# One graph layer on one core: the last bias of the message network moves from a TensorE product into the node part, by GpSimd, from the fifth group of nodes on

## The reference

```
h   = relu([x[src], x[dst]] @ Wm1 + bm1)      # 256 wide
h   = relu(h @ Wm2 + bm2)
agg = segment_mean(h @ Wm3 + bm3, dst)        # mean over the edges of a node, 0 where it has none
upd = relu([x, agg] @ Wn1 + bn1) @ Wn2 + bn2
out = layernorm(x + (x + upd))
```

## Time and profile before

| what | value |
|---|---|
| median of three runs | 1202.36 us (1200.36 to 1205.51) |
| the profiled execution: its own time | 1202.66 us |
| the profiled execution: span | 1200.9 us |
| busy share of the span: PE, PEld, DVE, ACT, POOL | 97%, 96%, 80%, 62%, 64% |
| last layer, from the first group's counts (1106.9) to the end | 94 us |

### The profile page before, as it was taken

One profiled execution on the slowest core, in us unless ns is written; L12 is line 12 of the kernel. 1 busy time (PEld: TensorE's weight loads), 2 busy tenths in 40 slices (PEclk: granted clock), 3 DMA queues, 4 the chain that ended last, 5 costly groups with the idle time before them and its releaser, 6 DMA issues.

```text
span 1200.9 us, 33955 instructions
## 1 busy us (share of the span) xinstructions
PE 1170.1 (97%) x9614; PEld 1149.9 (96%) x9615; DVE 961.7 (80%) x2072; ACT 747.9 (62%) x1392; POOL 770.2 (64%) x814
## 2 busy tenths in 40 slices
PE   6889999999999999999999999999999999999996
PEld 6778999999999999999999999999999999999886
DVE  6775877788788878888888888888888888888676
ACT  3555666666666666666666666666666666664684
POOL 2067777777777777777777777777777777771000
PEclk9998999999999999999999999999999999999999
DMA  9776666666665666666666666566666666662022
GB/s 327 274 289 176 181 179 175 179 181 177 180 178 178 178 180 177 179 177 179 178 179 179 180 178 179 176 180 177 180 179 176 179 180 178 179 177 75 27 71 92
DMA packets 135605, 211.42 MB, mean 176 GB/s; under 512 B 24247, under 2 KB 102669, under 8 KB 134030
## 3 DMA queue, kind: packets, MB, share of 16 engines
q0 software_dynamic: 37536, 102.55, 29.9%
q1 hardware_dynamic: 98030, 108.43, 29.4%
HBM read 188.09 MB, written 22.80 MB: 176 GB/s over the span
## 4 chain that ended last, share of the span: by engine, by line
PE 94%; DVE 1%; SPq 1%; DMA 1%; issue 1%; POOL 0%; ACT 0%; DVEq 0%
PE bank L1442 46%; PE bank L1418 14%; PE bank L1329 8%; PE sums L1352 4%; PE sums L1346 4%; PE sums L1350 4%; PE sums L1354 4%; PE bank L1483 3%; PE sums L1496 2%; PE bank L1239 1%; DMA a_table<-work 1%; PE bank L1466 1%; PE bank L1224 1%; PE sums L1224 1%; PE bank L1479 0%
## 5 line engine op out<-in xcount | busy, mean ns | idle before, releaser
L635 POOL DMA_INDIRECT a_edge<-a_table,src_idx x782 | 750.8, 960 | 258.9 <-issue 155.3
L1442 PE MATMUL bank<-w,h 128*128 128x256 f32 x4692 | 620.8, 282 | 0.0
L1442 PEld LDWEIGHTS bank<-w,h 128*128 128x128 f32 x4692 | 584.5, 189 | 0.0
L737 ACT ACTIVATE h<-bank 128x512 fp32r<-128x512 f32 x391 | 233.9, 598 | 324.7 <-PE bank L1329 321.8
L1111 DVE SCALAR_TENSOR_TENSOR h<-bank,h 128x512 fp32r<-128x512 f32 x391 | 269.4, 689 | 121.7 <-ACT h L737 85.7
L1123 DVE SCALAR_TENSOR_TENSOR h_lo<-bank,h_hi 128x512 fp32r<-128x512 f32 x391 | 266.7, 682 | 0.0
L726 ACT COPY bank<-b_bc 128x512 f32<-128x512 f32 x391 | 231.6, 592 | 42.9 <-DVE h_lo L1123 38.2
L1418 PE MATMUL bank<-ident,a_edge 128*128 128x128 f32 x1564 | 235.4, 273 | 5.7 <-DVE onehot_t L1028 3.9
L745 ACT ACTIVATE h_hi<-bank 128x512 fp32r<-128x512 f32 x391 | 232.9, 596 | 2.9 <-PE bank L1442 2.9
L1028 DVE TENSOR_SCALAR onehot_t<-rel,node_half 128x256 fp32r<-128x256 int16 x391 | 143.8, 368 | 57.8 <-DMA rel<-rel_dram 40.6
L1329 PE MATMUL bank<-onehot_t,b_win 128*128 128x256 f32 x782 | 189.9, 324 | 0.0
(11 more groups left out here) (190 smaller groups left out, 681.9 us busy)
## 6 DMA issues: line engine op xcount, KB each, us to landing
b_win<-b_table SPq DMA_DIRECT2D x391, 128.0 KB
rel<-rel_dram SPq DMA_DIRECT2D x196, 128.0 KB
a_edge<-a_table,src_idx POOLq DMA_INDIRECT x782
a_table<-work SPq DMA_DIRECT2D x12, 512.0 KB, 4.6
b_table<-work SPq DMA_DIRECT2D x5, 1024.0 KB, 6.0
b_table<-h SPq DMA_DIRECT2D x4, 1024.0 KB, 5.1
f_x<-in_x SPq DMA_DIRECT2D x12, 256.0 KB, 4.7
b_table<-a_edge SPq DMA_DIRECT2D x3, 1024.0 KB, 5.9
```

What stands on the lines that cost most here:

```text
L635: pool.indirect_dma_start(a_edge[:, b % R * TB + t, :], None, a_table, bass.IndirectOffsetOnAxis(ap=src_idx[:, b * TB + t:b * TB + t + 1], ...
L737: act.activation(h1[:, k % U, 0, :], bank[k % 2][:, :], ACT.Relu).then_inc(s_h1h, 1)
L1442: ins = pe.matmul(to, h1[:, j, a, h * EB + t * P:h * EB + (t + 1) * P], w2[:, b, h, :], start=False, stop=(a == 1 and h == KH - 1), skip_g ...
```

## The change

For groups 0 to 3 nothing changes in the arithmetic. From group 4 on (BY_ROW = 4) the mask row's transposes (L1467), its copy (L771) and its products with `b3_rows` (L1479) are left out. In their place `hx` itself gets mask times bm3 @ Wn1[128:256] added, by GpSimd, before ACT puts it into the banks. For that the mask of all nodes is made once (DVE), transposed (PE), copied (ACT), stored to DRAM by five transfers and loaded back spread over 128 partitions, 512 nodes at a time. The first three loads are issued by SP, the others by ACT. The diff, cut to its core:

```
+        b3_cols = sb("b3_cols", [P, KH * 2], F32)
+        f_mask, f_rows_by_4, f_rows = carve(P), carve(P), carve(P)
+        f_mask_bc = a_edge[:, 0:6, :].rearrange("p (k q) h -> p k (q h)", k=3)
+        BY_ROW = 4
+        def load_mask(e, g):
+            n = size(g) * P
+            e.dma_start(f_mask_bc[:, g % 3, 0:n], mask_dram[g * GW * P:g * GW * P + n].partition_broadcast(P)
+                        ).then_inc(s_mb[g % 3], 16)
 sync, behind the first three load_x_again:
+            whole = mask_dram[0:(NW - 1) * P].rearrange("(g n w a) -> w g n a", n=GW, w=GW, a=QUARTER)
+            sp.wait_ge(s_mc, 2)
+            for w in range(GW):
+                sp.dma_start(whole[w], f_rows_by_4[w:NW - 1:GW, :].rearrange("g (n a) -> g n a", n=GW)
+                             ).then_inc(s_ms, 16)
+            sp.dma_start(mask_dram[(NW - 1) * P:NW * P].rearrange("(o p) -> o p", o=1), f_rows[NW - 1:NW, :]
+                         ).then_inc(s_ms, 16)
+            sp.wait_ge(s_ms, 16 * (GW + 1))
+            for g in range(BY_ROW, BY_ROW + 3):
+                load_mask(sp, g)
 gpsimd, behind the gathers and the memsets of f_row (with f_mask cleared before them):
+            pool.wait_ge(s_hxa, 2 * NG)
+            pool.wait_ge(s_b3c, 1)
+            for g in range(BY_ROW, NG):
+                pool.wait_ge(s_mb[g % 3], 16 * mask_loads(g))
+                if g > BY_ROW:
+                    pool.wait_ge(s_hm, KH * (g - BY_ROW))
+                for h in range(KH):
+                    pool.tensor_scalar(f_part[h][:, 0:size(g) * P], f_mask_bc[:, g % 3, 0:size(g) * P],
+                                       b3_cols[:, 2 * h:2 * h + 1], None, ALU.mult).then_inc(s_hp, 1)
+                for h in range(KH):
+                    pool.wait_ge(s_hp, KH * (g - BY_ROW) + h + 1)
+                    at = hx[h][:, g * GW * P:(g * GW + size(g)) * P]
+                    pool.tensor_tensor(at, at, f_part[h][:, 0:size(g) * P], ALU.add).then_inc(s_hm, 1)
 scalar:
             def put_hx(g):
+                if g >= BY_ROW:
+                    act.wait_ge(s_hm, KH * (g - BY_ROW + 1))
+                    if size(g + 3):
+                        load_mask(act, g + 3)
...
-                    act.copy(f_row[g % 2][0:2, 0:n * P], bank[F_ROW][0:2, 0:n * P]).then_inc(s_fr, 1)
+                    if g < BY_ROW:
+                        act.copy(f_row[g % 2][0:2, 0:n * P], bank[F_ROW][0:2, 0:n * P]).then_inc(s_fr, 1)
+                    if g == 0:
+                        act.wait_ge(s_mt, 1)
+                        act.copy(f_rows_by_4[:, :]..., bank[F_UPD][:, 0:P]...).then_inc(s_mc, 1)
+                        act.copy(f_rows[:, :], bank[F_UPD][:, 0:P]).then_inc(s_mc, 1)
 vector, in copy_wc and behind means(0):
+                dve.tensor_copy(b3_cols[:, :], bank[0][:, 0:KH * 2]).then_inc(s_b3c, 1)
+            dve.tensor_scalar(f_mask[:, 0:NW], agg3[:, 0:NW, H:H + 1]..., 1.0, None, ALU.min).then_inc(s_mk, 1)
 tensor, beside the product of bm3 (L1297):
+                    for h in range(KH):
+                        pe.matmul(bank[0][:, 2 * h:2 * h + 2], wn1[:, 1, h * P:(h + 1) * P], b3_col[:, :],
+                                  start=True, stop=True)
 tensor, in the last layer:
-                        pe.wait_ge(s_fr, g)
+                        pe.wait_ge(s_fr, min(g, BY_ROW))
...
-                        ins = pe.transpose(by_nodes(bank[F_ROW][0:2, :], g, w), f_mean[:, k, w, H:HC], ident[:, :])
+                        if g < BY_ROW:
+                            ins = pe.transpose(by_nodes(bank[F_ROW][0:2, :], g, w), f_mean[:, k, w, H:HC],
+                                               ident[:, :])
...
                         keep_busy(bank[F_UPD][:, :], 9)
+                        pe.wait_ge(s_mk, 1)
+                        pe.transpose(bank[F_UPD][:, 0:P], f_mask[:, :], ident[:, :]).then_inc(s_mt, 1)
...
-                        pe.matmul(to, b3_rows[:, h * P:(h + 1) * P], f_row[j][:, 0:n], start=False, stop=False,
-                                  skip_group_check=True)
+                        if g - 1 < BY_ROW:
+                            pe.matmul(to, b3_rows[:, h * P:(h + 1) * P], f_row[j][:, 0:n], start=False, stop=False,
+                                      skip_group_check=True)
...
                     if g >= 3:
                         pe.wait_ge(s_fy, g - 2)
+                    else:
+                        pe.wait_ge(s_mc, 2)
```

More of the change, by code:

```diff
@@ L58, in gnn_layer @@
     rel_dram = nc.dram_tensor("rel_dram", [NB, EB], I16, kind="Internal").ap()
+    mask_dram = nc.dram_tensor("mask_dram", [NW * P], F32, kind="Internal").ap()
     mm_dram = nc.dram_tensor("mm_dram", [NB, 2], I32, kind="Internal").ap()
@@ L203, in gnn_layer @@
         f_row = [h1[:, k, 0, :] for k in range(2)]
+        f_mask, f_rows_by_4, f_rows = carve(P), carve(P), carve(P)
+        f_mask_bc = a_edge[:, 0:6, :].rearrange("p (k q) h -> p k (q h)", k=3)
+        f_part = (a_edge[:, 6:8, :].rearrange("p q h -> p (q h)"),
+                  rel[:, :, :].rearrange("p c e -> p (c e)").bitcast(F32))
+        BY_ROW = 4
         F_ROW, F_UPD = 5, 4
@@ L219, in gnn_layer @@
         s_b3 = sem("s_b3_parts")
+        s_b3c = sem("s_b3_columns")
         s_w2s = sem("s_w2_split")
@@ L293, in gnn_layer @@
         s_fr = sem("s_mask_row")
+        s_mz = sem("s_mask_zeroed")
+        s_mk = sem("s_mask_made")
+        s_mt = sem("s_mask_transposed")
+        s_mc = sem("s_mask_rows_copied")
+        s_ms = sem("s_mask_stored")
+        s_mb = [sem(f"s_mask_spread{k}") for k in range(3)]
+        s_hp = sem("s_masked_b3")
+        s_hm = sem("s_hx_with_masked_b3")
         s_fh = sem("s_hidden_product")
@@ L379, in f_hid, with mask_loads @@
             return agg[:, at:at + size(g) * P]
+        def mask_loads(g):
+            return sum(j % 3 == g % 3 for j in range(BY_ROW, g + 1))
+        def load_mask(e, g):
+            n = size(g) * P
+            e.dma_start(f_mask_bc[:, g % 3, 0:n], mask_dram[g * GW * P:g * GW * P + n].partition_broadcast(P)
+                        ).then_inc(s_mb[g % 3], 16)
         def by_dve(g):
@@ L638, in _ @@
                                             ).then_inc(s_g[b % R], 16)
+            pool.memset(f_mask[:, :], 0.0).then_inc(s_mz, 1)
             pool.wait_ge(s_w2, LAG)
@@ L770, in _ @@
                         act.wait_ge(s_frz, 2)
-                    act.copy(f_row[g % 2][0:2, 0:n * P], bank[F_ROW][0:2, 0:n * P]).then_inc(s_fr, 1)
+                    if g < BY_ROW:
+                        act.copy(f_row[g % 2][0:2, 0:n * P], bank[F_ROW][0:2, 0:n * P]).then_inc(s_fr, 1)
+                    if g == 0:
+                        act.wait_ge(s_mt, 1)
+                        act.copy(f_rows_by_4[:, :].rearrange("p (n a) -> p n a", n=GW),
+                                 bank[F_UPD][:, 0:P].rearrange("p (a n) -> p n a", n=GW)).then_inc(s_mc, 1)
+                        act.copy(f_rows[:, :], bank[F_UPD][:, 0:P]).then_inc(s_mc, 1)
                 n = size(g - 1)
@@ L1157, in _ @@
             means(0)
+            dve.wait_ge(s_mz, 1)
+            dve.tensor_scalar(f_mask[:, 0:NW], agg3[:, 0:NW, H:H + 1].rearrange("p w o -> p (w o)"), 1.0, None, ALU.min
+                              ).then_inc(s_mk, 1)
             for g in range(NG + 4):
@@ L1465, in _ @@
                         for h in range(KH):
-                            pe.transpose(by_nodes(bank[h], g, w), f_mean[:, k, w, h * P:(h + 1) * P], ident[:, :])
-                        ins = pe.transpose(by_nodes(bank[F_ROW][0:2, :], g, w), f_mean[:, k, w, H:HC], ident[:, :])
+                            ins = pe.transpose(by_nodes(bank[h], g, w), f_mean[:, k, w, h * P:(h + 1) * P],
+                                               ident[:, :])
+                        if g < BY_ROW:
+                            ins = pe.transpose(by_nodes(bank[F_ROW][0:2, :], g, w), f_mean[:, k, w, H:HC],
+                                               ident[:, :])
                     ins.then_inc(s_fmt, 1)
@@ L1474, in _ @@
                     pe.wait_ge(s_flo, 2 * g)
-                    pe.wait_ge(s_fr, g)
+                    if g - 1 < BY_ROW:
+                        pe.wait_ge(s_fr, g)
                     pe.wait_ge(s_fse, 2 * g)
```

1 line of the change is left out of this document (added).

## The result

| | before | after |
|---|---|---|
| median, us (runs, lowest to highest) | 1202.43 (6, 1200.36 to 1205.51) | 1190.77 (6, 1186.38 to 1197.62) |
| ratio | | 0.9911 [0.9891, 0.9931] |
| profiled execution, us (span) | 1202.66 (1200.9) | 1197.62 (1195.8) |
| edge loop, first to last batch, us | 1006.3 | 1006.8 |
| last layer, us | 94.0 | 87.4 |

The change made the kernel 11.7 us faster. Taken again in a second comparison the same kernel had 1193.96 us against 1201.53 (four executions, 1185.3 to 1197.7): 7.6 us faster. Over both, the median of its ten executions is 1193.5 us, and they spread over 12.4 us, those of the kernel before over 5.2 in the first. The execution with the profile is next to the longest of the ten, and that turns out to matter.

The account below looks back on a forecast made before the run. PE was taken to be full and to bound the last layer. Its saving of 7.3 us, plus 0.1 for an added transposition and 0.2 for hold-up, gave -7.0 us: forecast 1195.5 us, range 1193.9 to 1200.3.

Parts of the forecast that it names:

- The prologue: Ahead of the edge loop: two two-column products and a four-column DVE copy cost 0, or 0.3 us if on the path.
- TensorE's term: Last layer: dropping 33 mask-row transposes (3.6 us) and 16 b3_rows products (3.7) saves 7.3 us; one added transposition costs 0.1.
- The overlapped price of a transpose: Last layer, PE: a mask-row transpose costs 0.11 us on the chain, not its 273 ns duration, because matmuls overlap.
- The mask's way round: Storing the mask to DRAM and loading it back: first mask in place at 1121 to 1125.5 us, 1123 taken.
- ACT: Last layer: ACT loses a 0.5 us copy, gains a 0.43 us DMA issue in six groups, keeps 0.4 us idle; cost 0.
- rivals C and D: Last layer: C, first masked group late, 1198.7 us, chance 0.08; D, ACT bound by six DMA issues, 1197.7, chance 0.07.
- GpSimd's multiply by a column: Last layer, GpSimd's one-input instruction of 128x512: 0.55 us, range 0.5 to 1.0, bounded from a memset and half a cast.
- The add: Last layer, GpSimd's two-input instruction of 128x512: 1.0 to 1.2 us, not below 0.53 and not above 2.1.
- Rival A: Last layer: GpSimd holds up DVE at four places, 1.07 us a group, 3.6 us lost in all; 1199.0 us, chance 0.30.
- hold-up: Last layer: DVE slowed by GpSimd's arithmetic, 0.2 us allowed in all, since GpSimd idles some 2.3 us of a period.
- Rival B: Last layer: slow GpSimd adds of 1.6 us make DVE the bound, 4 us slower, 1206.4 us; chance 0.05.

Follow-up runs that it names:

- f0: The changed kernel again, with nothing altered, timed in a second comparison: 1193.96 us, ratio 0.9948; its profiled execution took 1185.3 us.
- e2: The changed kernel with b3_cols allocated behind work, so all other tensors keep their old addresses: 1193.44 us, ratio 0.9927.
- e3: The changed kernel without GpSimd's multiplies and adds (bm3's share left out from the fifth group on), masks, loads and waits kept: 1189.56 us, ratio 0.9885.
- f3: The kernel before with an unused 32-byte tensor where the change has b3_cols, run a second time for its profile: 1192.18 us, ratio 0.9949.
- e1: The kernel before with an unused tensor of 32 bytes per partition where the change has b3_cols, first run: 1193.45 us, ratio 0.9953.
- k2: The changed kernel with GpSimd's order in a group made multiply, add, multiply, add: 1187.25 us, ratio 0.9891.
- k5: The changed kernel with b3_cols allocated behind work and GpSimd's order made multiply, add, multiply, add: 1197.17 us, ratio 0.996.
- g1: The changed kernel with GpSimd's multiply by a column written as a multiply of two tensors, one a broadcast: 1195.77 us, ratio 0.9982.
- h3: The changed kernel with b3_cols allocated behind work and GpSimd's multiply written as one of two tensors: 1204.27 us, ratio 1.0023.
- f1: The kernel before with 32 unused bytes right before h1, moving h1 and what lies behind it: 1197.28 us, ratio 0.9955.
- f2: The kernel before with bn1_col allocated behind onehot, moving the tensors between by 32 bytes but not h1: 1200.79 us, ratio 0.9998.
- k1: The changed kernel with b3_cols allocated behind work and GpSimd's adds replaced by two more multiplies by a column: 1198.51 us, ratio 0.9969.

## Why the prediction was wrong, by its own steps

**The step that failed** is "The prologue. ... Cost 0", and with it the silent assumption that the edge loop is the same loop. The work that the step looked at did cost nothing that shows: the first matmul of L1442's kind starts at 92.4 us before and at 92.1 to 93.5 in after, f0, e2 and e3. What it did not look at is that a tensor of four columns is allocated there, ahead of h1. That made the loop up to 11 us shorter in after (f0) and 12 in the kernel before (f3). The shift alone gives 1193.45 and 1192.18 us (e1, f3), 8 and 9 us less than without it. Two more pairs that differ in the addresses alone say the same: k2 lies 9.9 us under k5, and g1 8.5 under h3. The pair of the change itself is the weak one: e2, without the shift, has 1193.44 us, after 1190.77 in one comparison and 1193.96 in the other. There the shift gives the executions near 1186 us, which e2 (1192.9 to 1195.2) lacks, and the others end at the gathers.

A second, smaller part of the miss is not explained: e2 itself lies 0.5 us under the range. Its last layer gains 6.3 us, less than the forecast's 7.0, and some 1.9 us come from elsewhere.

The mechanism is shown in part. It is addresses (e1, f3, e2). Moving h1 and those behind it does a part of it, moving only others nothing (f1, f2). It works through the distance of the matmuls of L1508, 118.2 ns down to 113.8 in two of four slots and to 117.4 in the others. By which rule is open: of pads of 0, 32, 64, 96 and 160 bytes only 32 gives two slots of 114 ns, and both rules that I tried, modulo 64 and modulo 128, were refuted. A longer modulus, or the distance between h1's slots, w2 and the tensors that other engines read and write meanwhile, was not tried.

**What stood.** TensorE's term: 7.3 less 0.1 predicted, 7.5 measured without GpSimd's arithmetic (e3), and the period there 5.69 us for 5.7. The overlapped price of a transpose, 0.11 us and not its 273 ns, was right. The mask's way round: GpSimd had the first mask at 1121.8 (1121 to 1125.5 predicted). ACT: an issue takes 0.33 to 0.35 us of its queue (0.43), and six gaps of 0.40 remain in its work, 2.4 us, which cost nothing. So rivals C and D did not occur.

**What was mis-sized.** GpSimd's multiply by a column: 0.55 us, range 0.5 to 1.0; it is 1.56 to 1.68. The memset and the cast from which it was bounded are no such operation, and "half a cast" was no upper bound. The add: 1.0 to 1.2; it is 1.27 to 1.34. So a group is 5.90 us and not 3.1 to 3.5, and GpSimd is never idle where "idle for some 2.3 us of a period" was written. The estimate of 1.1 to 1.2 us for the add, worked out from the 4497 ns for 2048 columns in the Trainium skill ("GPSIMD Engine Reference", section 3.1), is 0.1 to 0.2 us short of the measured 1.28.

**Rival A** was the right mechanism in kind, and its signs came: L1212 over 360 ns, no idle time before L1229, and TensorE waiting for L1253, 0.2 us in each of four groups. Two means of four are held in each group, by 0.95 us in sum (1.07 worked out), which uses up the idle 0.65 us; a period is then 5.90 us against e3's 5.69. Five periods are longer by this 0.2 us and one is 0.17 shorter, which makes the layer's 0.9 us. The small instructions are held where GpSimd's phase meets them (h3, k1, k5); in after L1204 and L1260 keep their 0.16 us. The forecast's 0.2 us for hold-up should have been 0.9; rival A's 3.6 was too much. Its premise that the four means pass together once the first is through is wrong: each is held by itself, two of four in after, all four in h3. That the means wait for the whole of GpSimd's instruction is right for the two-tensor form: all 81 end 0.15 us behind it. For the multiply by a column it is right in part: a mean that begins early in it is let in at about half of it, one that begins 0.97 us or more into it waits for its end, and one between passes. So the Trainium skill's "SBUF — State Buffer", section "Who interferes with whom", by which the later one waits for the whole of the other, agrees with the two-tensor forms, and with that multiply only in part.

**Rival B** did not come, though GpSimd is as busy as it supposed and more. h3 shows how near it was: with a GpSimd group of 4.7 us, all of the two-tensor form, the last layer is 3.0 us longer than before.

**The sum, corrected.** Last layer -7.5 + 0.9 = -6.6 us. Edge loop by execution: -10.9 (f0's profile) to +0.5 (after's), since its batch is now bound by either TensorE, 2.545 us on the mean of the four slots, or two gathers, 2.51 us at 950 ns each and 2.58 at 983. What makes a gather longer is DVE's L1103 at its start; why that meeting is more frequent and later in one execution than in another stays open.

## What to carry to other kernels

List what an edit allocates, not only what it issues: a new tensor ahead of a matmul's operands can move a loop that the edit doesn't touch, and one more variant with the tensor allocated last separates the two at the price of one run. Price work for a vector engine in two columns, its duration and what it does to the instructions of its neighbour; a faster form can be the dearer one (1.04 us against 1.56 here, and 9 us longer in h3's last layer than in e2's). And look for a second resource close to a loop's bound: here TensorE's 2.545 us a batch met gathers of 2.51 to 2.58, the gain ended there in some executions, and the spread of the times grew from 5 to 12 us.

## What the hardware showed that was not expected

- GpSimd, f32, 128x512: multiply by a per-partition column 1.56 to 1.68 us, add of two tensors 1.27 to 1.34, multiply of two tensors (one a broadcast) 1.04 to 1.17. With 128 columns the first two take 0.60 and 0.45. The form with one tensor is the slowest.
- A mean on DVE (128x258, 0.35 us) that begins under a two-tensor instruction of GpSimd's ends 0.15 us behind it, up to 1.38 us long (81 of 81). A multiply by a column has an opening: a mean that begins 0.75 to 0.87 us into it takes 0.34 us, and earlier or later ones are held (k1 and six more profiles).
- The other way round, most gather issues on GpSimd that begin under DVE's one-hot L1103 end 0.82 us behind it, and take 1.0 to 1.2 us instead of 0.95 (205 of 227 in after, 185 of 193 in f0).
- While DVE and GpSimd both have no idle time, the period of the last layer is the length of GpSimd's group: 5.90 us (e2), 6.12 (k5), 6.38 (k1). Which of the two sets it cannot be told from these runs.
- Twelve identical matmuls start 113.8 or 118.2 ns apart, by where in SBUF their operands lie, at a granted clock of 1.00.
- A gather's issue on GpSimd is 950 ns (960 to 983 on the mean) and the gap to the next 0.305 us. In this loop that is a second bound, 2.51 to 2.58 us a batch beside TensorE's 2.573 before and 2.545 after.
